# One ScalarE copy per weight slice in place of two, after the seventh step's value product

## The chip, the cores and the metric

The kernel runs on one core of a Trainium2 chip. The metric is the device time of one launch in microseconds, lower is better; the time before is the median of 3 runs.

## The reference, cut to what matters

One block of a Perceiver: a cross attention of 64 latents to 1601 context rows (plus the 64 latents), a small self attention, and a mixture of four feed-forward experts. The change lies in the stage of the cross attention, but the data it touches are the weights of the two later parts.

```
x = x + xattn(ctx (16,1601,256), layernorm(x (16,64,256)), mask, ...)
        q, k, v in 16 heads of 64;  w = softmax(q k^T + mask);  out = (w v) Wout
x = x + attn(layernorm(x), W_q, W_k, W_v, W_o, ...)        # 16 heads of 16, causal
x = x + ffn(layernorm(x), w1, w2, ...)                     # 4 experts, top 2, hidden 1024
```

## The kernel before

All arithmetic is float32, and a matmul on full precision is made of three: each operand is kept as a high part (float32 rounded for the matmul, made by a ScalarE copy) and a low part (operand minus high part, by VectorE or GpSimd), and `split_pair` issues high*high, high*low, low*high. It is the line L249 of most matmul rows.

The 16 batches of the cross attention run in the block `block_1`, one after the other. The 16 heads are 8 pairs `i`, and the keys are 13 chunks of 128. Each engine walks the same written list of events; the lists are made by `plan_x` (the first part of a batch) and `plan_y` (the second), 13 steps `c` each. In the first part of batch b the scores of pairs 0 to 3 of batch b are computed together with the value product of pairs 4 to 7 of batch b - 1. The events that matter here:

- `A(i, j)`: TensorE makes a quarter of the scores of pair i (`s_bank<-late,qkT`, 6 matmuls). VectorE adds the mask and takes the maximum (L926, `CUSTOM_DVE_ANT_0 prob<-s_bank,bias`); after the fourth quarter it makes `negmax` (L931).
- `E(i)`: ScalarE takes the exponential of pair i (L860, `prob<-prob,negmax`, 1665 columns). It waits for `negmax`.
- `P(i)`: VectorE divides by the sum: a reciprocal (L936) and a multiplication of 1665 columns, SBUF to SBUF (L938, `prob<-prob,rsum`).
- `Q(i)`: ScalarE and VectorE split the query-key operand of pair i (L844, then L907 `qkT<-qk,qkT`, whose inputs both lie in SBUF).
- `T(h, c)`: TensorE transposes chunk c of four pairs' probabilities into one of two PSUM banks (L994, `t_bank<-ident,prob`, 4 transposes); ScalarE copies the high part out (L838, `probT<-t_bank`); VectorE makes the low part (L902). The next-but-one transpose waits until L902 has freed the bank. `T(0, 0)` at the end of the first part reads pairs 0 to 3 and so waits for `P(3)`.
- `V(h, c)`: TensorE multiplies that chunk by the values (`o_bank<-probT,val`, 6 matmuls). It waits for L902 of `T(h, c)`.
- `N(g)`: the split of the values (L878 on ScalarE, L955 on VectorE). `S(g)`: `BATCH_NORM_STATS2` of the next batch's rows (L330). `O(h)`: the outputs leave their banks (L867, L943).
- `W`: one sixteenth of all later weights, 128 x 1280 float32 in `w_raw`, is split in passing: ScalarE writes the high part to `w_split[:, 0]` (L832; the profile names this tile `late_y`), GpSimd the low part (L807, one subtraction over 1280 columns, which reads `w_raw` and the high part), and SyncE stores both to `w_scratch` at the end of its own list for the batch.

ScalarE, VectorE and TensorE each execute their events strictly in the list's order. On GpSimd the list is short: the mask (L352), the W subtraction (L807), then the preparation of the next batch, which begins by waiting for the last statistics. On SyncE the load of `w_raw` comes first in a batch, the store of the split last.

In the middle batches the order of the first part from step 5 on is: A(2,1) P(1) A(2,2) W0 T(1,7) V(1,5) | T(1,8) V(1,6) S(4) | A(2,3) E(2) A(3,0) Q(4) A(3,1) P(2) T(1,9) V(1,7) N(1) | T(1,10) V(1,8) | A(3,2) A(3,3) E(3) W1 T(1,11) V(1,9) | P(3) T(1,12) V(1,10) S(0) | V(1,11) | T(0,0) V(1,12) S(1), then O(1). Bars divide the steps.

Of the kernel before, what the change touches and what calls it, by code (L numbers as in the profile page):

```python
# [20 lines left out]
ACT = mybir.ActivationFunctionType  # L21
# [32 lines left out]
WPART = WALL // B  # L54
# [10 lines left out]
X_UNITS = (0, 0, 0, 3, 4, 2, 0, 3, 0, 2, 0, 0, 0)  # L65
Y_UNITS = (0, 2, 2, 2, 2, 3, 0, 2, 0, 0, 0, 0, 0)

X_AT = {"W": (5, 9), "P3": 10, "Y0": 1, "N0": 3, "N1": 7, "S4": 6, "S0": 10, "S1": 12}
Y_AT = {"P7": 9, "Y1": 2, "N2": 0, "N3": 0, "S2": 3, "S3": 3, "H": (3, 3, 5, 6, 8, 9, 10)}
H_CHUNKS = ((13, 0, 1), (2, 3), (4, 5), (6, 7), (8, 9), (10, 11), (12,))  # L70

# [1 line left out]
def plan_x(has_a, has_b, has_next):  # L73

    ev = []
    units = [(i, j) for i in range(4) for j in range(4)]
    at = 2
    if has_a:
        ev += [("K", 0, 0), ("K", 1, 0), ("Q", 0), ("K", 0, 1), ("K", 1, 1)]
    for c in range(CH):  # L80
        if has_a:
            if c == 1:
                ev += unit_events(0, 0, 0)
            if c == 2:
                ev += [("K", 0, 2), ("K", 1, 2)] + unit_events(0, 1, 0)
            if c == 3:
                ev += [("K", 0, 3), ("K", 1, 3)]
            for i, j in units[at:at + X_UNITS[c]]:
                ev += unit_events(i, j, 0)
            at += X_UNITS[c]  # L90
            if c in X_AT["W"] and has_a:
                ev += [("W", X_AT["W"].index(c))]
            if c == X_AT["P3"] and has_b:
                ev += [("P", 3)]
            if c == 12 and has_b:
                ev += [("T", 0, 0)]
        if has_b:
            if c + 2 < CH:
                ev += [("T", 1, c + 2)]
            ev += [("V", 1, c)]  # L100
            if c == X_AT["Y0"]:
                ev += [("Y", 0)]
            if has_a:
                ev += [("N", g) for g in (0, 1) if c == X_AT[f"N{g}"]]
            if has_next:
                ev += [("S", g) for g in (4, 0, 1) if c == X_AT[f"S{g}"]]
    if has_b:
        ev += [("O", 1)]
    if has_a:
        ev += [("C",)]  # L110
    return ev
# [31 lines left out]
def unit_events(i, j, first):  # L143
    ev = [("A", i, j)]
    if j == 0 and i < PAIRS - 1:
        ev += [("Q", i + 1)]
    if j == 1 and i > first:
        ev += [("P", i - 1)]
    if j == 3:
        ev += [("E", i)]  # L150
    return ev


def has_next(y):
    return ("S", 2) in y
# [17 lines left out]
def load_y(sp, ysplit, y_scratch, rt, y_in):  # L173
    for q in range(2):
        sp.dma_start(ysplit[:, rt % YRING, q, :, :, :].bitcast(F32).rearrange("p a b l -> p a (b l)"),
                     y_scratch[q, :, :, 2 * rt:2 * rt + 2, :].rearrange("p a b l -> p a (b l)")
                     ).then_inc(y_in[rt % YRING], 16)


def load_split(sp, to, w_scratch, at, arrived):  # L180
    k, width = to.shape[1], to.shape[3]
    for q in range(2):
        sp.dma_start(to[:, :, q, :].bitcast(F32), w_scratch[q].rearrange("p n c -> p (n c)")[:, at:at + k * width]
                     .rearrange("p (k n) -> p k n", k=k)).then_inc(arrived, 16)
# [27 lines left out]
def wait(eng, sem, batch, k, c):  # L212

    assert batch.turn is None or batch.least(k, c) > 0
    if batch.least(k, c) > 0:
        eng.wait_ge(sem, batch.lin(k, c))
# [8 lines left out]
def periods(eng, step):  # L225

    step(Batch(0), X_FIRST, Y_FIRST)
    step(Batch(1), X_MID, Y_MID)
    with eng.Fori(0, B - 3) as turn:
        step(Batch(2, turn), X_MID, Y_MID)  # L230
    step(Batch(B - 1), X_LAST, Y_LAST)
    step(Batch(B), X_END, [])
# [441 lines left out]
def block_1(nc, ins, F, y_scratch, w_scratch, shared, used, ctx):  # L674

    W = shared

    def sb(name, shape, dt):
        return ctx.enter_context(nc.sbuf_tensor(name, shape, dt))
# [4 lines left out]
    def sem(name):  # L684
        return ctx.enter_context(nc.semaphore(name))
# [11 lines left out]
    w_raw = sb("w_raw", [P, WPART], F32)  # L697
    w_split = W["w_split"]
# [25 lines left out]
    w_raw_in, w_high, w_low = sem("w_raw_in"), sem("w_high"), sem("w_low")  # L724
# [5 lines left out]
    @block.sync  # L730
    def _(sp):
        def load_q_mask(n, index):

            wait(sp, mask_done, n, 2, 0)
            wait(sp, q_done, n, 8, 0)
            if n.turn is None and n.off == 1:

                for s in range(QK_RING):
                    sp.wait_ge(F.qk_out[s], 16 * (4 * PAIRS // QK_RING))
            F.load_q(sp, index)  # L740
            sp.dma_start(F.mask8[:, :], F.mask[index, :].partition_broadcast(P)).then_inc(mask_in, 16)

        def store_y(b, h, e, index):

            sp.wait_ge(t_done, b.use(e) + 1)
            for q in range(2):
                sp.dma_start(y_scratch[q, :, 4 * h:4 * h + 4, index, :],
                             ystage[:, h, q, :, :].bitcast(F32)).then_inc(y_out[h], 16)

        def load_w(n, index):  # L750

            wait(sp, w_low, n, 1, 0)
            sp.dma_start(w_raw[:, :], ins["wall"][:, index, :]).then_inc(w_raw_in, 16)

        def store_w(n, index):
            wait(sp, w_low, n, 1, 1)
            sp.dma_start(w_scratch[:, :, index, :].rearrange("q p c -> p q c"), w_split[:, :, :].bitcast(F32)).then_inc(w_out, 16)

        def step(b, x, y):
            nxt = Batch(b.off + 1, b.turn)  # L760
            if ("W", 0) in x:
                load_w(b, b.lin(1, 0))
            if b.turn is None and b.off == 0:
                for name in ("bqk", "bv", "bo"):
                    sp.dma_start(W[name][:, :], ins[name].partition_broadcast(P)).then_inc(W["c_in"], 16)
                for name in ("causal", "vmask", "headmask"):
                    sp.dma_start(W[name][:, :], ins[name]).then_inc(W["c_in"], 16)
                sp.dma_start(W["rot"][:, :, :], ins["rot"]).then_inc(W["c_in"], 16)
            if b.off == B:

                sp.wait_ge(score_out, 32 * B)
                load_split(sp, W["wout"], w_scratch, WCOLS["wout"][0], W["self_in"][0])
                sp.wait_ge(w_out, 16 * B)
                for h in range(2):
                    sp.wait_ge(y_out[h], 32 * 4)
                load_y(sp, W["ysplit"], y_scratch, 0, W["y_in"])
                sp.wait_ge(val_done, 4 * B)
                sp.dma_start(W["stage"][:, 0:RT, :], ins["x"].rearrange("(t p) d -> p t d", p=P)).then_inc(W["x_in"], 16)
                load_split(sp, W["wqk"], w_scratch, WCOLS["wqk"][0], W["self_in"][1])
                load_y(sp, W["ysplit"], y_scratch, 1, W["y_in"])  # L780
            if has_next(y):
                F.load_centre(sp, nxt, nxt.lin(1, 0))

                wait(sp, val_done, nxt, 4, -3)
            if ("Y", 0) in x:
                store_y(b, 0, ("Y", 0), b.lin(1, -1))
            if has_next(y):
                for g in range(4):
                    F.load_rows(sp, nxt, nxt.lin(1, 0), g)
            if ("Y", 1) in x + y:  # L790
                store_y(b, 1, ("Y", 1), b.lin(1, -1))
            if has_next(y):
                load_q_mask(nxt, nxt.lin(1, 0))
            if ("W", 0) in x:
                store_w(b, b.lin(1, 0))
        periods(sp, step)


    @block.gpsimd
    def _(pool):  # L800
        def step(b, x, y):
            if ("Q", 0) in x and b.off > 0:
                F.mask_bias(pool, b)
            if ("W", 0) in x:

                wait(pool, w_high, b, 2, 2)
                pool.tensor_tensor(w_split[:, 1, :], w_raw[:, :], w_split[:, 0, :].bitcast(F32), ALU.subtract  # L807
                                   ).then_inc(w_low, 1)
            if has_next(y):
                F.prepare(pool, Batch(b.off + 1, b.turn))  # L810
        periods(pool, step)
# [3 lines left out]
    def _(act):  # L815
        def half(b, events):
            for e in events:
# [10 lines left out]
                if kind == "W":  # L828
                    wait(act, w_raw_in, b, 16, 16)
                    wait(act, w_out, b, 16, 0)  # L830
                    s = slice(e[1] * WPART // 2, (e[1] + 1) * WPART // 2)
                    act.activation(w_split[:, 0, s], w_raw[:, s], ACT.Copy).then_inc(w_high, 1)  # L832
                if kind == "T":
                    when, c = e[1:]
                    slot, need = value_bank(min(when, 1), c)
# [1000 lines left out]
```

## Time and profile before

| | us |
|---|---|
| median of 3 runs (2013.17 to 2013.38) | 2013.21 |
| the profiled execution, its own time | 2012.02 |
| its span in the trace | 2009.3 |
| TensorE matmul busy | 1862.3 (93%) |
| TensorE weight load busy | 1622.6 (81%) |
| VectorE busy | 1366.7 (68%) |
| ScalarE busy | 956.6 (48%) |
| GpSimd busy | 601.1 (30%) |
| period of a middle batch (GpSimd's L807 starts at 887.61, then at 984.38) | 96.8 |

Busy shares are of the span. In the tables of the trace, PE is the matmul side of TensorE, PEld its weight load, DVE is VectorE, ACT ScalarE, POOL GpSimd and SP SyncE. A timeline row gives the start in us from the span's start, the duration in us, the engine, the line of the kernel, the operation, the tile written and the tiles read, the shapes, and in brackets how long the engine had been idle and who released it. Rows of equal instructions that follow each other are merged, with their count behind x. Matmuls overlap, so the start of one row may lie before the end of the last. GpSimd's ends are rough.

### The profile page before, as it was taken

The page shows a single profiled execution, that of the slowest core. Times are in us where ns is not written, and L with a number is a line of the kernel's source. Part 1 is how long each engine was busy: PE and PEld are TensorE (multiplying, and loading weights), DVE is VectorE, ACT ScalarE, POOL GpSimd, SP SyncE. Part 2 cuts the span into 40 slices and gives each one's busy share as a digit, 9 for nine tenths or more (in the row PEclk, how much of TensorE's full clock was granted, in tenths as well). Part 3 has the DMA queues.
Part 4 walks back from the last instruction along what each step waited for, and adds up shares of the span by engine and source line. Part 5 has one row for each costly group of instructions (what it writes and reads, how often), then busy time and mean ns, then how long its engine had stood idle before and what let it go on. Part 6 is the DMA issues. An engine that isn't in the chain of part 4 may idle for free. (4 is left out here: it accounts for less than half of the span.)

```text
span 2009.3 us, 32957 instructions
## 1 busy us (share of the span) xinstructions
PE 1862.3 (93%) x10615; PEld 1622.6 (81%) x10615; DVE 1366.7 (68%) x3147; ACT 956.6 (48%) x1677; POOL 601.1 (30%) x647
## 2 busy tenths in 40 slices
PE   5889999999999999999999999999999987768998
PEld 4678888888888888888888888888888876656887
DVE  6576767676767777676767677767676635755656
ACT  4545455454545454545454545554545432225344
POOL 3433324241515151514141414242333004530000
PEclk9989999999999999999999999999999998969999
DMA  7821303121212120212121212122130056002221
GB/s 280 262 83 35 94 20 94 27 84 29 82 29 82 29 82 29 82 39 72 42 72 39 72 44 73 48 72 58 53 89 10 32 148 209 23 1 74 84 93 55
DMA packets 168939, 146.88 MB, mean 73 GB/s; under 512 B 104848, under 2 KB 144688, under 8 KB 168880
## 3 DMA queue, kind: packets, MB, share of 16 engines
q1 hardware_dynamic: 168880, 146.12, 24.2%
q8 instruction: 34, 0.56, 0.1%
q14 instruction: 25, 0.20, 0.0%
HBM read 97.85 MB, written 48.25 MB: 73 GB/s over the span
## 5 line engine op out<-in xcount | busy, mean ns | idle before, releaser
L249 PE MATMUL o_bank<-probT,val 128*128 128x512 f32 x2496 | 685.4, 410 | 16.9 <-DVE probT L902 14.3
L249 PE MATMUL s_bank<-late,qkT 128*128 128x416 f32 x3072 | 626.7, 354 | 10.9 <-DVE qkT L907 9.1
L249 PEld LDWEIGHTS s_bank<-late,qkT 128*128 128x128 f32 x3072 | 569.1, 188 | 39.9 <-issue 10.9
L249 PEld LDWEIGHTS o_bank<-probT,val 128*128 128x128 f32 x2496 | 438.7, 189 | 101.5 <-DVE probT L902 20.9
L860 ACT ACTIVATE prob<-prob,negmax 128x1665 f32<-128x1665 f32 x128 | 216.0, 1688 | 374.0 <-DVE negmax L931 374.0
L902 DVE TENSOR_TENSOR probT<-t_bank,probT 128x512 fp32r<-128x512 f32 x416 | 283.0, 687 | 152.2 <-ACT probT L838 148.1
L838 ACT ACTIVATE probT<-t_bank 128x512 fp32r<-128x512 f32 x416 | 242.7, 591 | 231.9 <-PE t_bank L994 230.2
L926 DVE CUSTOM_DVE_ANT_0 prob<-s_bank,bias 128x416 f32<-128x416 f32 x512 | 294.9, 585 | 47.0 <-PE s_bank L249 45.5
L994 PE MATMUL t_bank<-ident,prob 128*128 128x128 f32 x1664 | 251.8, 274 | 31.4 <-DVE prob L938 23.9
L994 PEld LDWEIGHTS t_bank<-ident,prob 128*128 128x128 f32 x1664 | 205.0, 141 | 76.5 <-issue 22.8
L807 POOL TENSOR_TENSOR late_y<-w_raw,late_y 128x1280 fp32r<-128x1280 f32 x16 | 46.8, 2923 | 631.9 <-ACT late_y L832 631.9
L938 DVE TENSOR_SCALAR prob<-prob,rsum 128x1665 f32<-128x1665 f32 x128 | 188.4, 1472 | 4.6
L907 DVE TENSOR_TENSOR qkT<-qk,qkT 128x256 fp32r<-128x256 f32 x128 | 58.9, 460 | 113.7 <-ACT qkT L844 113.7
L393 POOL TENSOR_TENSOR stage<-stage 128x1024 f32<-128x1024 f32 x48 | 126.1, 2627 | 28.5 <-ACT stage L338 28.5
L394 POOL TENSOR_TENSOR stage<-stage,g 128x1024 f32<-128x1024 f32 x48 | 124.8, 2600 | 3.8
L338 ACT ACTIVATE stage<-stage,shift,rstd 128x256 f32<-128x256 f32 x224 | 119.9, 592 | 1.6 <-POOL shift L375 1.2
L897 DVE TENSOR_TENSOR ystage<-t_bank,ystage 64x256 fp32r<-64x256 f32 x64 | 27.0, 422 | 103.3 <-ACT ystage L827 102.9
L249 PEld LDWEIGHTS t_bank<-outT,wv 128*128 128x128 f32 x768 | 91.7, 194 | 5.5 <-issue 2.7
L249 PE MATMUL hbank<-xn2T,ffn_w 128*128 128x512 f32 x384 | 90.7, 393 | 5.1 <-ACT stage L1562 5.1
L249 PE MATMUL t_bank<-outT,wv 128*128 128x128 f32 x768 | 90.6, 275 | 2.3 <-DVE outT L943 2.3
L249 PEld LDWEIGHTS hbank<-xn2T,ffn_w 128*128 128x128 f32 x384 | 71.2, 188 | 23.1 <-ACT stage L1562 8.5
L1562 ACT ACTIVATE stage<-hbank,ffn_b 128x512 f32<-128x512 f32 x64 | 43.9, 688 | 79.0 <-PE hbank L249 70.5
(198 smaller groups left out, 1975.7 us busy)
## 6 DMA issues: line engine op xcount, KB each, us to landing
stage<-in_ctx SPq DMA_DIRECT2D x48, 512.0 KB, 3.8
w_scratch<-late_y SPq DMA_DIRECT2D x16, 1280.0 KB, 6.3
qk<-qk_scratch SPq DMA_DIRECT2D x16, 1024.0 KB, 6.8
ffn_w<-w_scratch SPq DMA_DIRECT2D x16, 1024.0 KB, 7.4
w_raw<-in_wall SPq DMA_DIRECT2D x16, 640.0 KB, 6.9
qk_scratch<-qk_own SPq DMA_DIRECT2D x16, 512.0 KB, 3.9
qk_scratch<-wraw SPq DMA_DIRECT2D x16, 512.0 KB, 4.3
y_scratch<-ystage SPq DMA_DIRECT2D x64, 128.0 KB, 2.1
```

Of the source, the lines that this page charges most:

```text
L249: mm = pe.matmul(out, weights(a), moving(b), start=first and n == 0, stop=last and n == 2)
L338: act.activation(self.raw[s, c, :], self.raw[s, c, :], ACT.Identity, bias=self.shift[s, m:m + 1], scale=self.rstd[s, m:m + 1]).then_inc(se ...
L393: link(eng.tensor_tensor(rows, rows, raw[:, 13:14, :].to_broadcast([P, 4, D]), ALU.subtract))
L394: eng.tensor_tensor(rows, rows, g1[:, :].unsqueeze(1).to_broadcast([P, 4, D]), ALU.mult).then_inc(self.keys_done, 1)
L807: pool.tensor_tensor(w_split[:, 1, :], w_raw[:, :], w_split[:, 0, :].bitcast(F32), ALU.subtract).then_inc(w_low, 1)
L838: act.activation(probT[:, slot, 0, :], bank[:, :], ACT.Copy).then_inc(t_high, 1)
L860: act.activation(prob[:, i, :], prob[:, i, :], ACT.Exp, bias=negmax[:, i:i + 1], accum_out=psum_[:, i:i + 1]).then_inc(exp_done, 1)
L902: dve.tensor_tensor(probT[:, slot, 1, :], bank[:, :], probT[:, slot, 0, :].bitcast(F32), ALU.subtract).then_inc(t_done, 1)
L907: dve.tensor_tensor(qkT[:, i % 2, :, 1, :], qk32[:, i, :, :, :].rearrange("p k h l -> p k (h l)"), qkT[:, i % 2, :, 0, :].bitcast(F32), AL ...
L926: apart(dve.tensor_tensor_reduce(out=prob[:, i, s], in0=s_bank[j][:, 0:QTR], in1=W["bias"][:, s], scale=1.0, scalar=NEG, op0=ALU.add, op1= ...
L938: dve.tensor_scalar(prob[:, i, :], prob[:, i, :], rsum[:, i:i + 1], None, ALU.mult).then_inc(prob_done, 1)
L994: mm = pe.transpose(bank[:, t * P:(t + 1) * P], prob[:, 4 * h + t, c * P:(c + 1) * P], ident[:, :])
```

## The change

The two halves of the high-part copy (640 columns each, at steps 5 and 9) become one copy of 1280 columns at step 6. In batches that have a value product, it stands behind `V(1, 6)`; in the first batch, which has none, it stands where the first half stood. GpSimd's subtraction waits for one signal in place of two, and so can start when that copy is done.

```diff
--- before.py
+++ after.py
@@ -65,7 +65,7 @@
 X_UNITS = (0, 0, 0, 3, 4, 2, 0, 3, 0, 2, 0, 0, 0)
 Y_UNITS = (0, 2, 2, 2, 2, 3, 0, 2, 0, 0, 0, 0, 0)
 
-X_AT = {"W": (5, 9), "P3": 10, "Y0": 1, "N0": 3, "N1": 7, "S4": 6, "S0": 10, "S1": 12}
+X_AT = {"W": 6, "P3": 10, "Y0": 1, "N0": 3, "N1": 7, "S4": 6, "S0": 10, "S1": 12}
 Y_AT = {"P7": 9, "Y1": 2, "N2": 0, "N3": 0, "S2": 3, "S3": 3, "H": (3, 3, 5, 6, 8, 9, 10)}
 H_CHUNKS = ((13, 0, 1), (2, 3), (4, 5), (6, 7), (8, 9), (10, 11), (12,))
 
@@ -88,18 +88,20 @@
             for i, j in units[at:at + X_UNITS[c]]:
                 ev += unit_events(i, j, 0)
             at += X_UNITS[c]
-            if c in X_AT["W"] and has_a:
-                ev += [("W", X_AT["W"].index(c))]
             if c == X_AT["P3"] and has_b:
                 ev += [("P", 3)]
             if c == 12 and has_b:
                 ev += [("T", 0, 0)]
+        if c == X_AT["W"] and has_a and not has_b:
+            ev += [("W",)]
         if has_b:
             if c + 2 < CH:
                 ev += [("T", 1, c + 2)]
             ev += [("V", 1, c)]
             if c == X_AT["Y0"]:
                 ev += [("Y", 0)]
+            if c == X_AT["W"] and has_a:
+                ev += [("W",)]
             if has_a:
                 ev += [("N", g) for g in (0, 1) if c == X_AT[f"N{g}"]]
             if has_next:
@@ -758,7 +760,7 @@
 
         def step(b, x, y):
             nxt = Batch(b.off + 1, b.turn)
-            if ("W", 0) in x:
+            if ("W",) in x:
                 load_w(b, b.lin(1, 0))
             if b.turn is None and b.off == 0:
                 for name in ("bqk", "bv", "bo"):
@@ -791,7 +793,7 @@
                 store_y(b, 1, ("Y", 1), b.lin(1, -1))
             if has_next(y):
                 load_q_mask(nxt, nxt.lin(1, 0))
-            if ("W", 0) in x:
+            if ("W",) in x:
                 store_w(b, b.lin(1, 0))
         periods(sp, step)
 
@@ -801,9 +803,9 @@
         def step(b, x, y):
             if ("Q", 0) in x and b.off > 0:
                 F.mask_bias(pool, b)
-            if ("W", 0) in x:
-
-                wait(pool, w_high, b, 2, 2)
+            if ("W",) in x:
+
+                wait(pool, w_high, b, 1, 1)
                 pool.tensor_tensor(w_split[:, 1, :], w_raw[:, :], w_split[:, 0, :].bitcast(F32), ALU.subtract
                                    ).then_inc(w_low, 1)
             if has_next(y):
@@ -828,8 +830,7 @@
                 if kind == "W":
                     wait(act, w_raw_in, b, 16, 16)
                     wait(act, w_out, b, 16, 0)
-                    s = slice(e[1] * WPART // 2, (e[1] + 1) * WPART // 2)
-                    act.activation(w_split[:, 0, s], w_raw[:, s], ACT.Copy).then_inc(w_high, 1)
+                    act.activation(w_split[:, 0, :], w_raw[:, :], ACT.Copy).then_inc(w_high, 1)
                 if kind == "T":
                     when, c = e[1:]
                     slot, need = value_bank(min(when, 1), c)
```

ScalarE's order in the middle batches, from the copy of `T(1, 6)` to the outputs, before. `late_y<-w_raw` is the W copy, `probT<-t_bank` the copy of a transposed chunk, `prob,psums<-prob,negmax` the exponential:

```order
L838 ACTIVATE probT<-t_bank 128x512
L832 ACTIVATE late_y<-w_raw 128x640
L838 ACTIVATE probT<-t_bank 128x512 x2
L860 ACTIVATE prob,psums<-prob,negmax 128x1665
L844 ACTIVATE qkT<-qk 128x2x128
L838 ACTIVATE probT<-t_bank 128x512
L878 ACTIVATE val<-stage 128x4x256
L838 ACTIVATE probT<-t_bank 128x512
L860 ACTIVATE prob,psums<-prob,negmax 128x1665
L832 ACTIVATE late_y<-w_raw 128x640
L838 ACTIVATE probT<-t_bank 128x512 x3
L867 ACTIVATE outT<-o_bank,x0T 128x512 x2
```

The same stretch of ScalarE's order after (the lines of the file are one further):

```order
L839 ACTIVATE probT<-t_bank 128x512 x3
L833 ACTIVATE late_y<-w_raw 128x1280
L861 ACTIVATE prob,psums<-prob,negmax 128x1665
L845 ACTIVATE qkT<-qk 128x2x128
L839 ACTIVATE probT<-t_bank 128x512
L879 ACTIVATE val<-stage 128x4x256
L839 ACTIVATE probT<-t_bank 128x512
L861 ACTIVATE prob,psums<-prob,negmax 128x1665
L839 ACTIVATE probT<-t_bank 128x512 x3
L868 ACTIVATE outT<-o_bank,x0T 128x512 x2
```

The copy between the exponential of pair 3 and the copies of `T(1, 11)`, `T(1, 12)` and `T(0, 0)` is gone, and the whole copy stands ahead of the exponential of pair 2.

In the first batch, before, ScalarE's order from the exponential of pair 1 on:

```order
L860 ACTIVATE prob,psums<-prob,negmax 128x1665
L844 ACTIVATE qkT<-qk 128x2x128
L832 ACTIVATE late_y<-w_raw 128x640
L860 ACTIVATE prob,psums<-prob,negmax 128x1665
L844 ACTIVATE qkT<-qk 128x2x128
L860 ACTIVATE prob,psums<-prob,negmax 128x1665
L832 ACTIVATE late_y<-w_raw 128x640
L844 ACTIVATE qkT<-qk 128x2x128
L838 ACTIVATE probT<-t_bank 128x512 x2
```

And after:

```order
L861 ACTIVATE prob,psums<-prob,negmax 128x1665
L845 ACTIVATE qkT<-qk 128x2x128
L833 ACTIVATE late_y<-w_raw 128x1280
L861 ACTIVATE prob,psums<-prob,negmax 128x1665
L845 ACTIVATE qkT<-qk 128x2x128
L861 ACTIVATE prob,psums<-prob,negmax 128x1665
L845 ACTIVATE qkT<-qk 128x2x128
L839 ACTIVATE probT<-t_bank 128x512 x2
```

Here the second half's place was ahead of the split of pair 5's operand. TensorE, VectorE, GpSimd and SyncE keep their instructions in the same order.

## Rows read from the trace of the kernel before

**Rows 1.** Waits of TensorE, whole run: us in total, times, longest.

```profile
PE t_bank L994 <- DVE prob L938: 23.9, 16, 7.1
...
PE o_bank L249 <- DVE probT L902: 14.3, 15, 1.0
```

**Rows 2.** Timeline of the end of one first part, a middle batch.

```profile
981.10 1.64 PE L249 MATMUL o_bank<-probT,val 128*128 128x512 f32 x6
...
981.88 1.69 ACT L860 ACTIVATE prob<-prob,negmax 128x1665 f32<-128x1665 f32 x1 [3.49 <-DVE negmax L931]
...
982.58 0.60 PE L994 MATMUL t_bank<-ident,prob 128*128 128x128 f32 x4
...
982.94 1.65 PE L249 MATMUL o_bank<-probT,val 128*128 128x512 f32 x6
...
983.57 0.72 ACT L832 ACTIVATE late_y<-w_raw 128x640 fp32r<-128x640 f32 x1
984.20 1.06 ACT L838 ACTIVATE probT<-t_bank 128x512 fp32r<-128x512 f32 x2
984.38 2.93 POOL L807 TENSOR_TENSOR late_y<-w_raw,late_y 128x1280 fp32r<-128x1280 f32 x1 [39.58 <-ACT late_y L832]
984.80 0.69 DVE L902 TENSOR_TENSOR probT<-t_bank,probT 128x512 fp32r<-128x512 f32 x1 [2.95 <-ACT probT L838]
...
985.55 1.67 PE L249 MATMUL o_bank<-probT,val 128*128 128x512 f32 x6 [0.96 <-DVE probT L902]
985.60 2.59 DVE L938 TENSOR_SCALAR prob<-prob,rsum 128x1665 f32<-128x1665 f32 x1
988.11 0.68 DVE L902 TENSOR_TENSOR probT<-t_bank,probT 128x512 fp32r<-128x512 f32 x1
...
988.33 0.63 PE L994 MATMUL t_bank<-ident,prob 128*128 128x128 f32 x4 [1.12 <-DVE prob L938]
...
988.84 1.66 PE L249 MATMUL o_bank<-probT,val 128*128 128x512 f32 x6
```

**Rows 3.** Timeline around step 6 of the same first part.

```profile
970.27 0.60 ACT L838 ACTIVATE probT<-t_bank 128x512 fp32r<-128x512 f32 x1 [1.24 <-PE t_bank L994]
...
973.66 1.69 ACT L860 ACTIVATE prob<-prob,negmax 128x1665 f32<-128x1665 f32 x1 [2.79 <-DVE negmax L931]
...
975.78 0.43 DVE L907 TENSOR_TENSOR qkT<-qk,qkT 128x256 fp32r<-128x256 f32 x1 [1.21 <-ACT qkT L844]
```

**Rows 4.** Timeline of the first batch, around the second half of the copy.

```profile
112.33 0.72 ACT L832 ACTIVATE late_y<-w_raw 128x640 fp32r<-128x640 f32 x1
112.95 0.40 ACT L844 ACTIVATE qkT<-qk 128x256 fp32r<-128x256 f32 x1
113.12 2.88 POOL L807 TENSOR_TENSOR late_y<-w_raw,late_y 128x1280 fp32r<-128x1280 f32 x1 [35.78 <-ACT late_y L832]
113.39 2.90 DVE L907 TENSOR_TENSOR qkT<-qk,qkT 128x256 fp32r<-128x256 f32 x1 [2.14 <-ACT qkT L844]
...
117.42 1.09 DVE L938 TENSOR_SCALAR prob<-prob,rsum 128x1665 f32<-128x1665 f32 x1
...
118.56 0.69 PE L994 MATMUL t_bank<-ident,prob 128*128 128x128 f32 x2 [7.14 <-DVE prob L938]
```

**Rows 5.** ScalarE's groups by shape: busy us, mean ns; idle before.

```profile
L878 ACT ACTIVATE val<-stage 128x1024 fp32r<-128x1024 f32 x48 | 50.5, 1054 | 9.5 <-PE o_bank L249 9.5
```

**Rows 6.** Timeline of a second part: VectorE while GpSimd works.

```profile
920.51 3.06 POOL L394 TENSOR_TENSOR stage<-stage,g 128x1024 f32<-128x1024 f32 x1
...
922.35 0.57 DVE L926 CUSTOM_DVE_ANT_0 prob<-s_bank,bias 128x416 f32<-128x416 f32 x1
...
923.03 0.15 DVE L923 CAST prob<-bias 128x1 f32<-128x1 bf16 x1
```

**Rows 7.** Stretches: us; busy of PE, PEld, DVE, ACT, POOL; PEclk; DMA.

```profile
120.00:125.00 5.00, 3.13 (x11) 2.08 (x10) 4.24 (x5) 4.53 (x7) 0.00 (x0) 0.50 0.17 17
440.00:1560.00 1120.00, 1084.95 (x6116) 965.87 (x6114) 792.35 (x1914) 578.97 (x1026) 375.60 (x392) 1.00 0.20 56
```

## The prediction

> **What bounds the kernel now.** I read the page first: TensorE's matmuls are busy 93% of the span, far ahead of every other engine. So only what TensorE loses counts, and the next view is its table of waits. Two entries there stand at every first part that has a value product and a weight slice (batches 1 to 15): transposes wait for the multiplication L938, 23.9 us in 16 times, of which one alone is 7.1, so (23.9 - 7.1) / 15 = 1.12 each; and value products wait for the low part L902, 14.3 us in 15 times, 0.95 each [rows 1]. Then the timeline of one such part, at the place where these waits lie [rows 2]. The period is 96.8 us (the table above), and equal longest and mean waits (1.0 and 0.95 for L902) say that the batches repeat each other; the sums below are made on this one and multiplied by 15.
>
> Follow the chain there. ScalarE starts the exponential of pair 3 at 981.88, then copies the second half of the weight slice at 983.57, and only then, at 984.20, copies `T(1, 11)` and `T(1, 12)`. VectorE had been idle for 2.95 and makes the low part at 984.80; TensorE, idle for 0.96, starts `V(1, 11)` at 985.55. Meanwhile the end of the weight copy has released GpSimd: its subtraction runs from 984.38 for 2.93. VectorE's multiplication for pair 3 starts at 985.60, inside it, and takes 2.59, where the same instruction takes 1.09 with GpSimd at rest (at 117.42) [rows 4]. It ends at 988.19, and `T(0, 0)`, which needs it, starts at 988.33 after 1.12 of idleness; `V(1, 12)` starts at 988.84. So both waits hang on the second half of the slice: one on its time on ScalarE, the other on the GpSimd work that it starts.
>
> **The change, part by part.** *The copy at step 9 goes.* The copies behind it start at 983.57 in place of 984.20, so 0.63 sooner; what was ready on TensorE (`T(1, 11)` ahead of 981.10) doesn't hold them. VectorE's L902 moves to 984.17, `V(1, 11)` to 984.92. TensorE could have started it 1.48 after `V(1, 10)`'s start (the distance from the value product at 981.10 to the transpose at 982.58), at 984.42, so some 0.5 of the loss stays there.
>
> *GpSimd's subtraction moves away from pair 3's multiplication.* That now starts at 985.60 - 0.63 = 984.97 and takes 1.09, to 986.06, in place of 988.19: 2.13 sooner. `T(0, 0)` can follow `V(1, 11)` at 984.92 + 1.48 = 986.40, with the multiplication done. L902 of `T(1, 12)` starts 0.08 before the multiplication's end, as it does now, at 985.98, and ends at 986.67. `V(1, 12)` can follow the transposes by 0.36 (982.58 to 982.94), at 986.76, just as its operand is there. Against 988.84 this is 2.08 sooner. If TensorE's lost time is taken from the wait entries alone, it is 0.63 + 1.12 = 1.75; the rest is the undisturbed spacing, which a stall breaks. I take 2.08, since starts are what the trace records, and 1.75 as the low bound. Behind `V(1, 12)` all engines are released by these same events, VectorE is 2.13 ahead, and no row ends on a transfer, so I expect it to be kept. For 15 batches: 15 x 2.08 = 31.2 (low bound 26.3).
>
> *One copy of 1280 columns at step 6.* No such copy is in the trace. From below it costs at least 1.05 (1024 columns [rows 5]), from above twice the halves' 0.72, 1.44; the line through 640 and 1024 columns gives 1.27, which I take. It can start about 0.5 after the copy of `T(1, 8)` at 970.27 and ends near 972.04 (972.2 at the most). The next instruction on ScalarE, the exponential of pair 2, waits for `negmax` until 973.66, after 2.79 of idleness [rows 3]. So the whole copy lies in that gap, with 1.5 to spare: cost nothing. Without this cover each microsecond would put off the exponential, behind it the split of pair 4's operand and the copies of `T(1, 9)`, and for these VectorE waits. The first half's old place at step 5 frees nothing: the copy behind it waited for TensorE.
>
> *GpSimd's subtraction at its new place.* Released near 972.1, it takes 2.93 and is done near 975.1. What VectorE does in it: scores of pairs 2 and 3 (L926), `negmax`, a cast of one column. In the second part two such instructions run within GpSimd's L394, at 0.57 and 0.15 [rows 6], unhindered. The instruction that does suffer, L907 (2.90 in the first batch, in GpSimd's 2.88 [rows 4], where it takes 0.43 alone [rows 3]), comes at 975.78, about 0.7 after the subtraction. The Trainium skill (SBUF — State Buffer, section Who interferes with whom) says that a VectorE instruction with two SBUF inputs, or in a 2-port mode, and a GpSimd one shut each other out for the whole instruction. It counts a cast among those that can enter such a mode, which would speak against the new place; the cast at 923.03 does not bear it out for this shape [rows 6]. On GpSimd nothing is queued behind the subtraction but the next batch's preparation, which waits for statistics that VectorE makes in the last steps; SyncE's store of the slice stands last in its list and doesn't move against the work around it, and the reload of `w_raw` follows it.
>
> *The first batch.* The second half at 112.33 goes, so L844 starts 0.62 sooner, at 112.33, and L907 at 112.77. The subtraction has run long before (released near 103), so L907 takes 0.43 in place of 2.90. Together 3.09, and pair 3's multiplication ends that much sooner; the transposes that wait for it move from 118.56 to 115.47 [rows 4]. TensorE is idle before them, 7.14, and its granted clock falls to 0.50, the level of 1.2 GHz, and is there from 120 to 125 [rows 7]. A shorter idle time may spare some of that: between nothing and one value product's 1.64. I take nothing.
>
> Sum: 31.2 + 3.1 = 34.3. On the profiled execution, 2012.02 - 34.3 = 1977.7; its own time is 1.2 under the median, so the median should be 2013.21 - 34.3 = 1978.9. The bounds: 26.3 + 3.1 = 29.4 gives 1983.8; 34.3 + 1.6 gives 1977.3.
>
> **The rivals.** *The multiplication stays long.* If the 2.59 of L938 has another cause than GpSimd, only the 0.63 on ScalarE is won, in 16 batches: 10.1, so 2003.1. For it: GpSimd's subtraction overlaps by start time only. Against: L907 in the first batch is 2.90 beside the same subtraction [rows 4]. Chance 0.04.
>
> *The wait moves with the subtraction.* If all of VectorE's work is held in the new place, the last scores of pair 2 begin only at 975.1, and with 0.8 for them and `negmax` the exponential of pair 2 starts at 975.9, 2.2 after its 973.66; I reckon 0.4 of that absorbed in gaps, and the exponential of pair 3 some 1.8 late. The copies of `T(1, 11)` then come at 983.57 + 1.8, and `V(1, 12)` at about 988.75, 0.1 sooner than before: 1.5 + 3.1 won, so 2008.6. Only L907 could really do this, if the subtraction began 0.7 later than I reckon. Chance 0.06.
>
> *Something else takes half.* Behind `V(1, 12)` VectorE is busy almost without gap (statistics, outputs, scores), and a step there could become what TensorE waits for. With half of the 31.2 given back, 1994.5. For it: how full VectorE is there. Against: it arrives 2.13 sooner itself. Chance 0.14.
>
> *The clock.* The other side: TensorE, less idle, is granted less. The loop now has the full level throughout at 1084.95 busy of 1120 [rows 7]. Work at 1.2 GHz takes twice the time, so it decides from 34.3 / 15 = 2.3 us of full-speed work per batch at that level; if 5 us of it fell to that level in each batch, as they do once from 120 to 125, 75 would be added, 40.7 net: 2053.9. Against: the one fall in these rows follows idleness, and the change has less. Chance 0.03.
>
> **How the numbers follow.** The forecast has 0.73, its own range 1976.5 to 1984. With the part of the third rival that lies nearest, 1976.5 to 1990 holds 8 in 10. 0.2% is 4 us, about what a measurement of this kernel can tell from no change. Faster: the forecast, the first and the third rival, and most of the second (which at 4.6 us is just beyond): 0.94. Within 0.2%: 0.03. Slower: 0.03.
>
> **What would show it.** In the profile after: L938 of pair 3 at 1.09 in every batch; TensorE's wait for L938 down to one of some 4 us in the first batch; its wait for L902 before `V(1, 11)` near 0.3; one L832 of about 1.27 per batch, in the idle time before the exponential of pair 2; L807 some 12 us sooner, with no L907 or L938 inside it; a period near 94.7. I am wrong if a VectorE row between 972 and 976 is longer than now, if L907 waits, or if TensorE shows a new wait in steps 7 to 12 or early in the second part.

## The result, and the profile after

The changed kernel takes 1981.13 us (median of 4 runs, 1977.47 to 1982.44) against 2013.3 (2013.17 to 2015.67): a ratio of 0.9835, 95% interval 0.9818 to 0.9852. It is 32.2 us faster; 1978.9 was forecast.

TensorE's waits after the change, whole run (us in total, times, longest):

```profile
PE o_bank L251 <- DVE probT L903: 5.0, 15, 0.3
...
PE t_bank L995 <- DVE prob L939: 4.0, 1, 4.0
```

The wait for the multiplication, now L939, is down from 16 times to the one of the first batch, 4.0 in place of 7.1, and the wait for the low part, now L903, from 14.3 us to 5.0 in its 15 times; both answer to [rows 1].

The end of a first part after, at the place of [rows 2]:

```profile
963.66 1.69 ACT L861 ACTIVATE prob<-prob,negmax 128x1665 f32<-128x1665 f32 x1 [3.49 <-DVE negmax L932]
...
964.72 1.65 PE L251 MATMUL o_bank<-probT,val 128*128 128x512 f32 x6
...
965.35 1.06 ACT L839 ACTIVATE probT<-t_bank 128x512 fp32r<-128x512 f32 x2
...
966.70 1.67 PE L251 MATMUL o_bank<-probT,val 128*128 128x512 f32 x6 [0.33 <-DVE probT L903]
966.75 1.09 DVE L939 TENSOR_SCALAR prob<-prob,rsum 128x1665 f32<-128x1665 f32 x1
...
968.21 0.60 PE L995 MATMUL t_bank<-ident,prob 128*128 128x128 f32 x4
...
968.56 1.65 PE L251 MATMUL o_bank<-probT,val 128*128 128x512 f32 x6
```

Times are read from the start of the exponential of pair 3. `V(1, 11)` follows its start by 966.70 - 963.66 = 3.04, before by 3.67. The multiplication takes 1.09, not 2.59, and no GpSimd row stands in the stretch. `T(0, 0)` has no wait. `V(1, 12)` comes 4.90 after the exponential's start, before 6.96: 2.06 sooner. A middle batch now takes 94.7 (`V(1, 11)` starts at 871.97, then at 966.70) in place of 96.8; the forecast named 94.7.

Step 6 after, at the place of [rows 3]:

```profile
952.54 1.27 ACT L833 ACTIVATE late_y<-w_raw 128x1280 fp32r<-128x1280 f32 x1
...
953.89 2.96 POOL L809 TENSOR_TENSOR late_y<-w_raw,late_y 128x1280 fp32r<-128x1280 f32 x1 [27.32 <-ACT late_y L833]
954.61 0.59 DVE L927 CUSTOM_DVE_ANT_0 prob<-s_bank,bias 128x416 f32<-128x416 f32 x1 [0.81 <-PE s_bank L251]
...
955.32 0.14 DVE L924 CAST prob<-bias 128x1 f32<-128x1 bf16 x1
955.44 1.69 ACT L861 ACTIVATE prob<-prob,negmax 128x1665 f32<-128x1665 f32 x1 [1.63 <-DVE negmax L932]
...
957.56 0.43 DVE L908 TENSOR_TENSOR qkT<-qk,qkT 128x256 fp32r<-128x256 f32 x1 [1.21 <-ACT qkT L845]
```

The one copy takes 1.27 and lies in the idle time ahead of the exponential of pair 2, of which 1.63 is left. GpSimd's subtraction runs from 953.89 to 956.85. The scores L927 (0.59) and the cast L924 (0.14) run within it at their usual length, and the operation with two inputs in SBUF, L908, starts 0.7 after its end, at 0.43.

The first batch after, at the place of [rows 4]:

```profile
112.05 1.69 ACT L861 ACTIVATE prob<-prob,negmax 128x1665 f32<-128x1665 f32 x1 [3.41 <-DVE negmax L932]
...
114.17 0.43 DVE L908 TENSOR_TENSOR qkT<-qk,qkT 128x256 fp32r<-128x256 f32 x1 [1.52 <-ACT qkT L845]
...
116.87 1.09 PE L995 MATMUL t_bank<-ident,prob 128*128 128x128 f32 x8 [4.03 <-DVE prob L939]
```

From the start of the exponential of pair 3 to the first transposes it is 4.82; before it was 7.92 (110.64 to 118.56): 3.10 sooner. L908 takes 0.43 in place of 2.90. TensorE's granted clock still falls to 0.50, the level of 1.2 GHz (from 118 to 124). But it is 0.99 from 116 to 118, and these 8 transposes take 1.09. Before, it was 0.52 from 116 to 118, ahead of them, and they took 1.97.

### The profile page after: what moved, and what is told of

Its sections match the earlier page's. It is cut to its first block and busy times, and to the rows that moved or that the text cites. A ratio compares the mean times of both kernels' runs of the same rounds, so it can differ in the third digit from the quotient of the medians.

```text
span 1977.0 us, 32926 instructions
## 1 busy us (share of the span) xinstructions
PE 1858.9 (94%) x10615; PEld 1623.8 (82%) x10615; DVE 1341.9 (68%) x3147; ACT 955.0 (48%) x1661; POOL 603.2 (31%) x647
## 5 line engine op out<-in xcount | busy, mean ns | idle before, releaser
L903 DVE TENSOR_TENSOR probT<-t_bank,probT 128x512 fp32r<-128x512 f32 x416 | 283.3, 687 | 142.4 <-ACT probT L839 138.4
L927 DVE CUSTOM_DVE_ANT_0 prob<-s_bank,bias 128x416 f32<-128x416 f32 x512 | 294.9, 586 | 47.6 <-PE s_bank L251 45.9
L995 PEld LDWEIGHTS t_bank<-ident,prob 128*128 128x128 f32 x1664 | 205.4, 141 | 53.1 <-DVE probT L903 15.3
L939 DVE TENSOR_SCALAR prob<-prob,rsum 128x1665 f32<-128x1665 f32 x128 | 165.9, 1296 | 4.6
L908 DVE TENSOR_TENSOR qkT<-qk,qkT 128x256 fp32r<-128x256 f32 x128 | 56.4, 440 | 113.1 <-ACT qkT L845 113.1
```

The lines of the kernel that those rows point to most:

```text
L903: dve.tensor_tensor(probT[:, slot, 1, :], bank[:, :], probT[:, slot, 0, :].bitcast(F32), ALU.subtract).then_inc(t_done, 1)
L908: dve.tensor_tensor(qkT[:, i % 2, :, 1, :], qk32[:, i, :, :, :].rearrange("p k h l -> p k (h l)"), qkT[:, i % 2, :, 0, :].bitcast(F32), AL ...
L927: apart(dve.tensor_tensor_reduce(out=prob[:, i, s], in0=s_bank[j][:, 0:QTR], in1=W["bias"][:, s], scale=1.0, scalar=NEG, op0=ALU.add, op1= ...
L939: dve.tensor_scalar(prob[:, i, :], prob[:, i, :], rsum[:, i:i + 1], None, ALU.mult).then_inc(prob_done, 1)
L995: mm = pe.transpose(bank[:, t * P:(t + 1) * P], prob[:, 4 * h + t, c * P:(c + 1) * P], ident[:, :])
```

## A measure for the stage

The runs of one kernel differ by 2.5 to 10 us from the fastest to the slowest. The later parts, which no change here touches, share in that: behind the cross attention's last `x0T` copy, the profiled executions take 430.5 to 437.7 us to the end of their spans. A stretch inside the cross attention is steadier: from the first to the last of the 16 copies `x0T`, of which each batch has one near the end of its first part. Its rows (duration min/median/max, first and last start), before and then after:

```profile
L950 DVE COPY x0T<-x0next x16: 159/170/170, 110.5 to 1574.3; 128x2 f32<-128x2 f32 x16
```

```profile
L951 DVE COPY x0T<-x0next x16: 159/169/170, 111.9 to 1541.8; 128x2 f32<-128x2 f32 x16
```

That is 1463.8 before and 1429.9 after, 33.9 less. The spans of the two profiled executions differ by 32.3. The missing 1.6 lies outside the stretch: the first copy is 1.4 later after the change (110.5 to 111.9), and so, by 2.1, was already the load of the first weight slice, issued ahead of any changed instruction (82.3 before, 84.4 after); the part behind the last copy is 0.2 longer.

The stretch has one unsteady piece itself, the first period, from the first `x0T` copy to the second. In it TensorE's clock falls once, and how long it stays down differs between kernels. In experiment 3 and after the change, whose middle batches take the same time, the first period is 104.2 and 103.2. So the table also gives the middle period: the distance from the third copy to the fifteenth, divided by 12. The experiments below are compared by it, by the stretch, and by their times with the interval. The ratios are against the kernel before as it ran beside each group: 2015.27 us for 1 to 4, 2013.57 for 5 to 7.

| kernel | time, us | ratio to before | stretch, us | against before | middle period, us |
|---|---|---|---|---|---|
| before | 2013.3 | | 1463.8 | | 96.77 |
| after | 1981.13 | 0.9835 (0.9818 to 0.9852) | 1429.9 | -33.9 | 94.73 |
| 1: subtraction after pair 3's exponential | 2001.76 | 0.9941 (0.9924 to 0.9957) | 1454.5 | -9.3 | 96.16 |
| 2: before, subtraction after pair 3's multiplication | 1989.59 | 0.9872 (0.9855 to 0.9888) | 1440.4 | -23.4 | 95.35 |
| 3: two halves at step 6 | 1977.75 | 0.9815 (0.9799 to 0.9831) | 1430.6 | -33.2 | 94.72 |
| 4: subtraction after pair 2's exponential | 2028.57 | 1.006 (1.004 to 1.0079) | 1478.0 | +14.2 | 97.99 (mixed, see there) |
| 5: one copy at step 9 | 2020.6 | 1.0034 (1.0021 to 1.0047) | 1473.0 | +9.2 | 97.31 |
| 6: copy of `T(1, 11)` ahead of pair 3's exponential | 1968.14 | 0.9777 (0.9763 to 0.979) | 1421.4 | -42.4 | 94.10 |
| 7: and that of `T(0, 9)` ahead of pair 7's | 1959.25 | 0.9732 (0.9719 to 0.9746) | 1410.7 | -53.1 | 93.51 |

## The experiments

The theory to test was that two things add up: GpSimd's subtraction no longer shuts out pair 3's multiplication (the larger part), and ScalarE reaches the copy of `T(1, 11)` 0.63 sooner. The rivals: one of the two does it all, or merging does.

### 1: the subtraction back in its old place

```diff
                 wait(pool, w_high, b, 1, 1)
+                wait(pool, exp_done, b, 8, 4)
```

> The changed kernel, but GpSimd's subtraction also waits for the exponential of pair 3, so that it runs about where it ran before the change; ScalarE's order stays the changed one. Theory (most of the gain is that the subtraction no longer shuts out pair 3's multiplication): the multiplication is stretched again, to end some 3.8 us after the subtraction's start; V(1,12) comes 1.35 later than in the changed kernel in 15 batches, and in the first batch the qkT subtraction is held for 2.5 more: 1981 + 22.7, about 2004. Rival (the freed time on ScalarE is the cause, GpSimd's place is not): 1981, multiplication at 1.09 or its length without effect.

Timeline of a first part's end in this kernel:

```profile
976.46 1.69 ACT L862 ACTIVATE prob<-prob,negmax 128x1665 f32<-128x1665 f32 x1 [3.49 <-DVE negmax L933]
...
978.32 2.92 POOL L810 TENSOR_TENSOR late_y<-w_raw,late_y 128x1280 fp32r<-128x1280 f32 x1 [38.94 <-ACT prob L862]
...
979.50 1.67 PE L251 MATMUL o_bank<-probT,val 128*128 128x512 f32 x6 [0.33 <-DVE probT L904]
979.55 2.58 DVE L940 TENSOR_SCALAR prob<-prob,rsum 128x1665 f32<-128x1665 f32 x1
...
982.28 0.63 PE L996 MATMUL t_bank<-ident,prob 128*128 128x128 f32 x4 [1.11 <-DVE prob L940]
```

ScalarE's copies and `V(1, 11)` come as early as in the changed kernel (3.04 after the exponential's start), but the subtraction starts at 978.32, the multiplication at 979.55 takes 2.58, and `T(0, 0)` waits 1.11 for it. The stretch loses 24.6 us of its 33.9. A middle batch takes 1.43 more than after the change (96.16, 94.73), where 1.35 was expected. So the place of GpSimd's work is the larger part, and the rival of ScalarE's time alone falls.

### 2: the old ScalarE order, the subtraction out of the way

```diff
                 wait(pool, w_high, b, 2, 2)
+                wait(pool, prob_done, b, 8, 4)
```

> The kernel before, both half copies in their old places, but GpSimd's subtraction also waits for pair 3's multiplication. Theory: the multiplication takes 1.09 and T(0,0) comes at the undisturbed spacing, while V(1,11) still waits 0.96: 1.45 per batch in 15 batches and 2.5 in the first, 24 us less than before, about 1989. The part that the ScalarE time brings is the remaining 8 to 10 us to 1981. Rival (VectorE's stretched instruction is not what TensorE waits for): 2013.

```profile
971.29 0.72 ACT L833 ACTIVATE late_y<-w_raw 128x640 fp32r<-128x640 f32 x1
...
973.27 1.68 PE L249 MATMUL o_bank<-probT,val 128*128 128x512 f32 x6 [0.96 <-DVE probT L903]
973.32 1.08 DVE L939 TENSOR_SCALAR prob<-prob,rsum 128x1665 f32<-128x1665 f32 x1
...
974.49 2.96 POOL L808 TENSOR_TENSOR late_y<-w_raw,late_y 128x1280 fp32r<-128x1280 f32 x1 [41.98 <-DVE prob L939]
...
974.78 0.60 PE L995 MATMUL t_bank<-ident,prob 128*128 128x128 f32 x4
```

The same place in this kernel: the half copy at 971.29 still stands ahead of the copies and `V(1, 11)` waits its old 0.96, but the multiplication takes 1.08, the subtraction follows at 974.49, and `T(0, 0)` has no wait. 23.4 us of the stretch are won, where 24 was expected, with every copy where it was before. What the ScalarE time adds in a middle batch is 95.35 - 94.73 = 0.62, where 0.63 was reckoned. The two parts add up. Alone, the ScalarE time wins 96.77 - 96.16 = 0.61 a batch (experiment 1), and the subtraction's new place wins 96.77 - 95.35 = 1.42 (this one). The sum is 2.03, and the change wins 96.77 - 94.73 = 2.04.

### 3: the move without the merge

```diff
-                wait(pool, w_high, b, 1, 1)
+                wait(pool, w_high, b, 2, 2)
...
-                    act.activation(w_split[:, 0, :], w_raw[:, :], ACT.Copy).then_inc(w_high, 1)
+                    for s in (slice(0, WPART // 2), slice(WPART // 2, WPART)):
+                        act.activation(w_split[:, 0, s], w_raw[:, s], ACT.Copy).then_inc(w_high, 1)
```

> The changed kernel with two half copies back to back at step 6 in place of the one copy. Theory (the place is all, merging is nothing because it lies in idle time): 1981, halves of 0.72, GpSimd's start 0.1 to 0.2 later, no new wait. Rival (one instruction fewer on ScalarE is worth something): 0.18 in 16 batches, 2.9 us, 1984.

```profile
952.55 1.36 ACT L834 ACTIVATE late_y<-w_raw 128x640 fp32r<-128x640 f32 x2
...
953.99 2.96 POOL L809 TENSOR_TENSOR late_y<-w_raw,late_y 128x1280 fp32r<-128x1280 f32 x1 [27.42 <-ACT late_y L834]
...
955.44 1.69 ACT L862 ACTIVATE prob<-prob,negmax 128x1665 f32<-128x1665 f32 x1 [1.53 <-DVE negmax L933]
```

Step 6 in this kernel: both halves take 1.36 together, GpSimd starts 0.10 later, and the exponential of pair 2 starts at 955.44, as it does after the change. A middle batch takes the same (94.72, 94.73). The stretch is 0.7 longer, by its first period, and the time is 3.4 shorter with intervals that overlap. One instruction fewer is worth nothing that these runs can tell.

### 4: the subtraction ahead of the qkT subtraction

```diff
                 wait(pool, w_high, b, 1, 1)
+                wait(pool, exp_done, b, 8, 3)
```

> The changed kernel, but GpSimd's subtraction also waits for the exponential of pair 2, so that it starts some 0.4 ahead of the qkT subtraction L908 (two inputs in SBUF). Theory (exclusion by GpSimd costs wherever VectorE has no slack): L908 takes 2.6 to 2.9, the exponential of pair 3 comes 2.1 later, V(1,12) about 2.1 later, in 15 batches, and 2.4 in the first: 2015, all of the gain lost. Rival (VectorE has enough gaps there, only the multiplication ahead of T(0,0) is critical): at most 1985.

```profile
983.12 1.69 ACT L862 ACTIVATE prob<-prob,negmax 128x1665 f32<-128x1665 f32 x1 [1.62 <-DVE negmax L933]
...
984.98 2.94 POOL L810 TENSOR_TENSOR late_y<-w_raw,late_y 128x1280 fp32r<-128x1280 f32 x1 [30.72 <-ACT prob L862]
...
985.24 2.96 DVE L909 TENSOR_TENSOR qkT<-qk,qkT 128x256 fp32r<-128x256 f32 x1 [1.21 <-ACT qkT L846]
...
993.49 1.69 ACT L862 ACTIVATE prob<-prob,negmax 128x1665 f32<-128x1665 f32 x1 [5.63 <-DVE negmax L933]
...
996.53 1.66 PE L251 MATMUL o_bank<-probT,val 128*128 128x512 f32 x6 [2.06 <-DVE probT L904]
...
998.38 1.65 PE L251 MATMUL o_bank<-probT,val 128*128 128x512 f32 x6
...
1000.23 3.64 PE L251 MATMUL s_bank<-late,qkT 128*128 128x416 f32 x18
```

The subtraction starts at 984.98, L909 at 985.24 and takes 2.96 in place of 0.43. The exponential of pair 3 starts 10.37 after that of pair 2, after the change 8.22: 2.15 later, and `V(1, 11)` waits 2.06. In the first batch the same wait holds the first `x0T` copy back by 2.5 (114.4, after the change 111.9). As far as that the expectation holds. But the kernel takes 2028.57 where 2015 was expected, and is slower than before. The rest is the clock. Another batch of the same run, and then the granted clock (the number ahead of the last two) of a stretch in each of the two batches:

```profile
898.09 1.76 PE L251 MATMUL o_bank<-probT,val 128*128 128x512 f32 x6 [2.07 <-DVE probT L904]
...
900.37 2.81 PE L251 MATMUL o_bank<-probT,val 128*128 128x512 f32 x6
...
903.37 3.65 PE L251 MATMUL s_bank<-late,qkT 128*128 128x416 f32 x18
```

```profile
900.00:904.00 4.00, 4.00 (x17) 3.37 (x16) 3.22 (x10) 1.39 (x3) 0.38 (x2) 0.63 0.00 0
...
998.00:1002.00 4.00, 4.00 (x24) 3.63 (x23) 4.00 (x11) 2.52 (x5) 0.36 (x2) 1.00 0.00 0
```

After nearly the same wait (2.07) the clock fell here: `V(1, 12)` takes 2.81 in place of 1.65, and from the start of `V(1, 11)` to the scores it is 5.28 in place of 3.70 (996.53 to 1000.23), 1.6 more. `V(1, 11)` waits 2.05 to 2.08 in each of the 15 batches. In five of them the granted clock is 1.00 in the 4 us that begin 1.5 behind its start, and the next `V(1, 11)` starts 96.84 to 96.87 later: 2.12 more than after the change, as expected. In the other ten it is 0.58 to 0.72; the next `V(1, 11)` comes 98.42 to 98.46 later in eight of these, and 99.44 later in the ninth. The stretch is 48.1 longer than after the change. 15 times 2.12 are 31.8 of it, and the remaining 16.3 go with the ten falls. My expectation had left them out. What decides between a fall and none after the same wait is not shown.

### 5: the merge without the move

```diff
-X_AT = {"W": (5, 9), "P3": 10, ...
+X_AT = {"W": 9, "P3": 10, ...
...
-            if c in X_AT["W"] and has_a:
-                ev += [("W", X_AT["W"].index(c))]
+            if c == X_AT["W"] and has_a:
+                ev += [("W",)]
```

(and the full copy and GpSimd's wait as in the change)

> The kernel before with one copy of 1280 columns at the old second place, step 9, none at step 5. Merging alone, without the move. Theory: the copies behind it start 0.55 later than before (1.27 in place of 0.72), GpSimd and pair 3's multiplication likewise: V(1,12) 0.55 later in 15 batches and 0.55 in the first, 2013 + 8.8 = 2022. Rival (merging is a gain of its own): 2013 or below.

```profile
990.30 1.26 ACT L831 ACTIVATE late_y<-w_raw 128x1280 fp32r<-128x1280 f32 x1
991.46 1.06 ACT L837 ACTIVATE probT<-t_bank 128x512 fp32r<-128x512 f32 x2
991.64 2.92 POOL L807 TENSOR_TENSOR late_y<-w_raw,late_y 128x1280 fp32r<-128x1280 f32 x1 [40.11 <-ACT late_y L831]
...
992.81 1.67 PE L249 MATMUL o_bank<-probT,val 128*128 128x512 f32 x6 [1.49 <-DVE probT L901]
992.86 2.58 DVE L937 TENSOR_SCALAR prob<-prob,rsum 128x1665 f32<-128x1665 f32 x1
...
995.59 0.63 PE L993 MATMUL t_bank<-ident,prob 128*128 128x128 f32 x4 [1.10 <-DVE prob L937]
```

The copy of 1.26 at the old second place puts off the copies of `T(1, 11)` and `T(1, 12)` by half a microsecond: `V(1, 11)` waits 1.49, and the multiplication is stretched to 2.58 as before. A middle batch takes 0.54 more (97.31, 96.77), where 0.55 was expected, and the stretch is 9.2 longer. Merged in the old place, the copy makes the kernel slower: the interval of its ratio, 1.0021 to 1.0047, leaves out 1.

### 6: what is left at this place

```diff
             if c + 2 < CH:
-                ev += [("T", 1, c + 2)]
+                late_e = [ev.pop()] if ev and ev[-1][0] == "E" and c in X_LATE_E else []
+                ev += [("T", 1, c + 2)] + late_e
```

with `X_LATE_E = (9,)`, on top of the changed kernel.

> The changed kernel, with ScalarE's copy of T(1,11) moved ahead of the exponential of pair 3 (nothing else in any order changes). Theory of what is left at this place: V(1,11) waits because the copy stands behind the exponential; ahead of it, it fits in ScalarE's idle time, the exponential starts at most 0.1 later, and the loss of 0.5 goes to 0.1: 15 x 0.4 = 6 less than the changed kernel, 1975. Rival (pair 3's multiplication, whose exponential is now 0.1 to 0.2 later, takes over the wait): 1981, with a wait for the multiplication ahead of T(0,0).

```profile
957.92 0.60 ACT L841 ACTIVATE probT<-t_bank 128x512 fp32r<-128x512 f32 x1 [3.07 <-PE t_bank L997]
...
958.41 1.68 ACT L863 ACTIVATE prob<-prob,negmax 128x1665 f32<-128x1665 f32 x1
...
959.39 3.05 PE L253 MATMUL o_bank<-probT,val 128*128 128x512 f32 x12
...
960.41 1.09 DVE L941 TENSOR_SCALAR prob<-prob,rsum 128x1665 f32<-128x1665 f32 x1
...
962.29 0.60 PE L997 MATMUL t_bank<-ident,prob 128*128 128x128 f32 x4
```

ScalarE copies `T(1, 11)` at 957.92, in its idle time, and the exponential of pair 3 follows at 958.41. `V(1, 10)` and `V(1, 11)` are now one run of 12 matmuls, and the multiplication (960.41, done at 961.50) is in time for `T(0, 0)` at 962.29. The stretch is 8.5 us shorter than after the change, 6 expected: from the start of `V(1, 10)` to `T(0, 0)` it is 2.90 where it was 3.49 (964.72 to 968.21), 0.59 less where 0.4 was expected. I had left 0.1 of the loss standing, which is gone too, and had put the undisturbed spacing of two value products at 1.48, where this run of two gives 3.05 - 1.65 = 1.40. A middle batch takes 0.63 less. The medians differ by 13.0. Of the spans' difference, 14.4, 4.7 lies behind the stretch (430.5 to the end of the span, after the change 435.2) and 1.2 ahead of it, where nothing was changed. The rival, a new wait for the multiplication, does not show.

### 7: the same in the second part

```diff
+        late_e = [ev.pop()] if ev[-1][0] == "E" and c in Y_LATE_E else []
         ev += [("T", 0, c + 2)] if c + 2 < CH else [("T", 2, c - 11)]
-        ev += [("V", 0, c)]
+        ev += late_e + [("V", 0, c)]
```

with `Y_LATE_E = (7,)`, on top of experiment 6.

> As the last, and in the second part the copy of T(0,9) also moved ahead of the exponential of pair 7, where TensorE waits 0.4 to 0.5 for the low part of T(0,9) in each of 15 batches. Theory: that wait goes too, 16 x 0.5 = 8 less than the last kernel: 1967. Rival (VectorE or the bank frees no earlier, as its low part waits for something else): as the last.

All that TensorE waits for between 240 and 1450 us in this kernel:

```profile
PE s_bank L255 <- DVE qkT L912: 5.4, 13, 0.4
```

The wait for a low part is gone there; one of 0.4 a batch is left. A middle batch takes 0.59 less than in experiment 6, which makes 8.9 in 15 batches, 8 expected. The stretch is 10.7 us shorter; some 1.8 of that lies in the first period (103.5, now 101.1), beyond these 0.59. Its clock came back sooner: the granted clock from 124 to 126 is 0.80, in experiment 6 it is 0.50. At 1959.25 us this kernel is the best of all, 0.9732 of before.

## Why the prediction was right, point by point

- *The copy at step 9 goes*: `V(1, 11)` was to come 0.63 sooner and came 0.63 sooner (3.67 to 3.04). Experiment 2 against the changed kernel gives 0.62 a batch.
- *GpSimd's subtraction moves away*: the multiplication was to take 1.09 and does. `T(0, 0)` was reckoned 1.48 behind `V(1, 11)` and is 1.51; `V(1, 12)` was to gain 2.08 and gained 2.06; the middle period shrank by 2.04. Experiments 1 and 2 show both ways that the subtraction's place is the cause. The low bound, 1.75 from the wait entries, was too low: the start-to-start spacing was the better measure.
- *The copy of 1280 columns*: reckoned at 1.27, measured 1.26 to 1.27, and it costs nothing in its gap.
- *The subtraction's new place*: reckoned to end 0.7 ahead of the qkT subtraction; it does (956.85, 957.56). Experiment 4 shows what this margin guards.
- *The first batch*: 3.09 reckoned, 3.10 measured at the first transposes. Of TensorE's idle time 4.03 is left, and the lower clock level comes all the same. I had taken nothing for the clock. The first period shrank by 5.6 (108.8 to 103.2), which is some 0.4 more than the 2.04 of a middle batch and these 3.10. It goes with the clock, which fell a little later.
- *Sum*: 34.3 reckoned, 33.9 in the stretch, 32.2 between the medians. That the stretch comes within 0.4 is in part luck: each of the 15 batches won 0.04 to 0.05 less than reckoned, 0.7 in all, and the first won some 0.4 more. Most of the rest to 32.2 is the later start of the stretch, which nothing in the change explains.

Of the rivals, *The multiplication stays long* and *Something else takes half* did not come, and neither did *The clock*. *The wait moves with the subtraction* was priced too low: made to happen by experiment 4 it ends at 2028.57, not at 2008.6. Of these 20 us, 16 go with the falls of the clock behind TensorE's longer wait, and 2.5 are the first batch's, which the experiment held back as well and the rival did not. The rival's own sum has a slip too: from 983.57 + 1.8 the chain of the change leads to 988.56 for `V(1, 12)`, not to 988.75, so it should have read 2005.9. I had kept the clock under a rival of its own, and tied it there to a busier TensorE; it came with an idler one.

The rule of the Trainium skill that was weighed (SBUF — State Buffer, section Who interferes with whom) agrees with experiments 4 and 1: the qkT subtraction, with two inputs in SBUF, took 2.96 in place of 0.43 and the multiplication 2.58 in place of 1.09, each begun within GpSimd's subtraction. Its remark on casts did not bite: the cast of one column ran at 0.14 within the subtraction.

## What to carry to other kernels

Work that is done in passing on two idle engines is not free where it stands: look at what its start and its end release. Here a half copy of 0.72 us cost 0.63 by itself and about 1.4 more because its end started a GpSimd operation just ahead of a VectorE operation that was then held: the multiplication took 2.59 in place of 1.09. Find the longest idle time of the copying engine that is followed by a stretch without such VectorE operations. Then look at what stands last ahead of each remaining wait: putting a short copy ahead of a long exponential whose input was not there yet, at two places, won another 1.2 us a batch, 19 us of the stretch.

## What the hardware showed beyond the expected

The exclusion works the other way too. The tile view of the weight slice after the change, ScalarE's and GpSimd's rows (duration min/median/max, first and last start):

```profile
L833 ACT ACTIVATE late_y<-w_raw x16: 1258/1266/1269, 103.1 to 1521.8; 128x1280 fp32r<-128x1280 f32 x16
L809 POOL TENSOR_TENSOR late_y<-w_raw,late_y x16: 2957/2957/3758, 104.4 to 1523.1; 128x1280 fp32r<-128x1280 f32 x16
```

The 3758 ns are the first batch's, where VectorE's multiplication of pair 1 had begun 0.17 ahead of the subtraction (104.22, 104.39). It cost nothing there: the subtraction ended at 108.15, and the next operation with two inputs in SBUF, L908 at 108.67, took its usual 0.42. And the granted clock can fall after a wait of TensorE of only 2.07, and stay up after one of 2.06 in another batch of the same run (experiment 4), so a wait of that length cost its own length in some batches and 1.6 us more in others. After shorter waits the clock stayed at 1.00 throughout the middle batches (240 to 1450 us): 0.95 and 1.12 before the change, 1.49 and 1.10 in experiment 5.
